# Two heads at once in a feature attention: maxima's rows handed over ahead of the query stores, and each query part stored once instead of once per use

## The chip, the cores and the metric

The kernel runs on one core of a Trainium2 chip. The metric is the device time of one execution in microseconds. A measured time is the median of several executions; one more execution was recorded by the hardware profiler, and every row shown below is from that one.

## The reference, cut to what matters

The program is a two-layer decoder block on x of 32 x 64 x 256 (2048 rows of 256, 16 tiles of 128 rows). It is six sublayers in a row: differential attention, feature attention, a selected low-rank feed-forward, a state-space layer, grouped attention and a mixture of experts. The change touches the second, and the end of the first, which prepares its first tiles. The second computes attention between features: the 64 rows of a sample are split into 8 heads of 8 rows, and each head has a 256 x 256 table of scores.

```python
def _L0_xattn_ref(q, k, v, W):           # q = layernorm(x), k = v = ctx, each (32, 64, 256)
    qh = q.reshape(B, H, D, Tq)          # H = 8 heads of D = 8 rows
    kh = k.reshape(B, H, D, Tk)
    vh = v.reshape(B, H, D, Tk)
    a = jnp.einsum('bhdq,bhdk->bhqk', qh, kh) * SCALE
    p = jax.nn.softmax(a, axis=-1)
    y = jnp.einsum('bhqk,bhdk->bhdq', p, vh).reshape(B, C, T)
    return jax.nn.selu(jnp.einsum('oc,bct->bot', W, y))
x = x + _L0_xattn_ref(layernorm(x), ctx, ctx, W)
```

A tile of 128 rows is two samples (b = 0, 1), so 16 heads, each with 256 x 256 scores.

## The kernel before, in words

**Scores from bf16 parts.** Queries and keys are float32, and the scores are made from three bf16 parts of each (high, middle, low). A product keeps six terms: the pairs of parts (0,0), (1,0), (2,0), (0,1), (1,1), (0,2) of query and key. The contraction of one head is then 6 terms x 8 rows = 48 rows. So the query stack has the parts in the order 0, 1, 2, 0, 1, 0 (`Q_TERMS`), the key stack in the order 0, 0, 0, 1, 1, 2 (`K_TERMS`). The stacks lie in SBUF with 48 rows of one head at partitions 0 to 47 and 48 rows of another at partitions 64 to 111 (two lanes), so that two heads are on the array at once. To bring the 8 rows of a head together from a tile's 128 partitions, each part goes through DRAM: `store` (line 176) writes a part to `q_parts` or `k_parts`, once for each of the six terms, and `load` (line 180) reads all 48 rows back, one DMA for each lane.

**Maxima.** The softmax needs each row's maximum ahead of the exponential. Head by head, TensorE first makes the scores with the queries on the output's partitions (`largest`, line 951), VectorE reduces them (`maximum`, line 783, two PSUM banks in turn), and GpSimd splits the 16 negated maxima of half a tile into three bf16 parts (`split_max`, lines 916 to 922). TensorE turns them into rows (`turn_max`, line 983), ScalarE copies these to SBUF (`max_to_rows`, line 832), and SyncE moves them by two DMAs into three more rows under the query stack (`max_to_stack`, line 747). There they meet three rows of ones in the key stack, so that the second product (`score`, line 956, 51 rows, keys on the partitions) has the maximum taken off, and ScalarE takes its exponential (line 838).

**The turn.** Each engine runs its own instruction list with semaphores between them, through `pipeline` (line 715): turns t = -1 to 16, of which -1 to 4 and 13 to 16 are unrolled and 5 to 12 lie in a loop. In turn t the engines work on several tiles:
- tile t + 3: x is normalised (VectorE line 113), split (GpSimd lines 905 to 911) and stored by SyncE (`store`, turns 1 to 12);
- tile t + 2: SyncE loads key and query stacks (`load`, turns 2 to 13);
- tile t + 1: `largest` and `maximum` for its 16 heads;
- tile t: `score`, exponentials, and the product with the values (`mix`, line 968);
- tile t - 1: output product (line 1036), SELU (ScalarE lines 861, 862, 872, then GpSimd lines 934 to 940, which end with x), and row statistics for the next sublayer (VectorE line 818, which waits for that x).

The 16 heads of a turn are eight groups, heads(0,0) to heads(0,3) and heads(1,0) to heads(1,3), with a `largest` and a `score` interleaved. All else of TensorE stands between two groups, in an order written by hand, and the lists of ScalarE and SyncE follow the same pattern. Two halves of maxima pass in each turn: `turn_max(t, 1)`, whose rows heads(1,0) of the same turn waits for, and `turn_max(t + 1, 0)`, whose rows heads(0,0) of the next turn waits for.

SyncE issues all DMAs in order. Before the change its turn is: load the context; wait for the maxima's rows of (t, 1) and issue their two DMAs; two key loads; wait until the tile's stores have landed; two query loads; six query stores; wait for the rows of (t + 1, 0) and issue their two DMAs.

## Time and profile before

| | us |
|---|---|
| median of 3 runs | 1390.13 |
| lowest, highest of them | 1388.1, 1390.63 |
| the profiled execution's own time | 1384.98 |
| its span (first to last instruction) | 1383.2 |
| feature attention in it, first matmul of line 951 to last of line 1036 | 252.0 to 500 |
| its mean granted TensorE clock | 0.962 of 2.4 GHz |

The profile names instructions by line and engine: PE is TensorE, PEld its weight loads, DVE VectorE, ACT ScalarE, POOL GpSimd, SP and SPq SyncE. "idle before <-releaser" is the time in which the engine waited ahead of the instruction, and what ended the wait.

### The profile page before, as it was taken

The numbers are of one execution on the slowest core, as the hardware profiler recorded it, in microseconds if no ns is written. First come the engines' busy times: TensorE is split into PE (matmuls) and PEld (weight loads), VectorE is DVE, ScalarE is ACT, GpSimd is POOL, SyncE is SP. The second block draws the span as 40 slices with busy tenths as digits, with TensorE's granted clock in tenths as the row PEclk, the third lists the DMA queues.
The fourth block names the chain that finished last, engine by engine and source line by source line (L and its number), as shares of the span: only waits on it lengthen the run. The fifth ranks groups of instructions, "written<-read, shape, count | busy, mean of one in ns | idle before, by whom it ended". The sixth has DMA issues, their size and how long they took to land. (4 is left out here: it accounts for less than half of the span.)

```text
span 1383.2 us, 27648 instructions
## 1 busy us (share of the span) xinstructions
PE 1231.3 (89%) x9980; PEld 970.1 (70%) x9996; DVE 987.4 (71%) x1869; ACT 705.4 (51%) x1457; POOL 455.3 (33%) x537
## 2 busy tenths in 40 slices
PE   4999998788888867889779999999997799999998
PEld 3776766233333335779657878787877799999998
DVE  4799987687777838788567777777866648655555
ACT  1555665287767854500156665656564364333332
POOL 1333543154444323457553424242322111112210
PEclk9999999699999989999899999999999899999999
DMA  5111025024333221000210000000000300000001
GB/s 177 32 26 35 24 69 134 23 61 106 87 82 84 53 65 45 1 0 0 90 56 4 4 7 4 8 4 8 4 5 0 93 24 25 24 24 24 2 1 62
DMA packets 64927, 54.52 MB, mean 39 GB/s; under 512 B 9192, under 2 KB 56904, under 8 KB 64456
## 3 DMA queue, kind: packets, MB, share of 16 engines
q1 hardware_dynamic: 64846, 53.42, 14.0%
q8 instruction: 53, 0.87, 0.3%
q14 instruction: 28, 0.23, 0.1%
HBM read 38.32 MB, written 14.68 MB: 38 GB/s over the span
## 5 line engine op out<-in xcount | busy, mean ns | idle before, releaser
L783 DVE TENSOR_REDUCE fa_neg_max<-psum 128x2 f32<-128x512 f32 x256 | 162.9, 686 | 38.9 <-PE psum L951 37.8
L838 ACT ACTIVATE fa_probs<-psum 128x1024 f32<-128x1024 f32 x128 | 130.9, 1024 | 45.2 <-PE psum L956 44.7
L1803 PE MATMUL psum<-mo_xT_high,mo_w_high 128*128 128x256 f32 x512 | 145.6, 284 | 2.4 <-DVE mo_xT_low L2631 2.2
L1803 PE MATMUL psum<-mo_xT_low,mo_w_high 128*128 128x256 f32 x512 | 145.2, 284 | 0.0
L1803 PE MATMUL psum<-mo_xT_high,mo_w_low 128*128 128x256 f32 x512 | 144.6, 282 | 0.0
L2463 ACT ACTIVATE mo_silu<-psum 128x256 f32<-128x256 f32 x128 | 49.0, 384 | 155.0 <-PE psum L1803 155.0
L2597 DVE TENSOR_TENSOR mo_mid<-mo_silu,psum 128x256 f32<-128x256 f32 x128 | 53.7, 420 | 92.8 <-ACT mo_silu L2463 92.7
L951 PE MATMUL psum<-stacks_k_stack,stacks_q_stack 48*128 48x256 bf16 x512 | 92.0, 290 | 29.1 <-DMA stacks_q_stack<-fa_max_rows 15.1
L1803 PEld LDWEIGHTS psum<-mo_xT_high,mo_w_high 128*128 128x128 f32 x512 | 97.4, 190 | 3.0 <-DVE mo_xT_low L2631 2.6
L1939 POOL TENSOR_TENSOR ga_probs<-ga_probs,ga_top 128x1024 f32<-128x1024 f32 x16 | 30.5, 1906 | 206.0 <-DVE ga_top L2093 206.0
L1803 PEld LDWEIGHTS psum<-mo_xT_low,mo_w_high 128*128 128x128 f32 x512 | 97.5, 190 | 0.0
L1803 PEld LDWEIGHTS psum<-mo_xT_high,mo_w_low 128*128 128x128 f32 x512 | 97.4, 190 | 0.0
L951 PEld LDWEIGHTS psum<-stacks_k_stack,stacks_q_stack 48*128 48x128 bf16 x512 | 32.7, 97 | 87.5 <-DVE fa_neg_max L783 42.3
L2404 POOL TENSOR_TENSOR mo_w_low<-mo_raw,mo_w_high 128x512 fp32r<-128x512 f32 x21 | 27.5, 1311 | 188.1 <-ACT mo_w_high L2438 188.1
L956 PE MATMUL psum<-stacks_q_stack,stacks_k_stack 51*128 51x256 bf16 x512 | 85.5, 283 | 0.3 <-DMA stacks_q_stack<-fa_max_rows 0.2
L1928 POOL TENSOR_TENSOR ga_q_scaled<-ga_q,ga_q_inv 128x1024 f32<-128x1024 f32 x32 | 70.1, 2190 | 38.2 <-ACT ga_q_inv L1970 38.2
L968 PE MATMUL psum<-fa_probs,fa_values 128*32 128x256 f32 x1024 | 71.8, 400 | 0.7 <-ACT fa_probs L838 0.6
L1963 ACT ACTIVATE ga_q_scaled<-ga_q 128x512 f32<-128x512 f32 x64 | 40.4, 632 | 62.6 <-DVE ga_q L2066 62.6
L1803 PE MATMUL psum<-mo_w_high,mo_mid_high 128*128 128x256 f32 x256 | 72.3, 282 | 0.0
L1803 PE MATMUL psum<-mo_w_low,mo_mid_high 128*128 128x256 f32 x256 | 71.9, 281 | 0.0
L1803 PE MATMUL psum<-mo_w_high,mo_mid_low 128*128 128x256 f32 x256 | 71.7, 280 | 0.0
L2262 PE MATMUL psum<-ga_w_o_high,ga_mixedT_high 128*128 128x256 f32 x256 | 63.2, 288 | 4.4 <-DVE ga_mixedT_low L2085 4.3
(419 smaller groups left out, 3584.2 us busy)
## 6 DMA issues: line engine op xcount, KB each, us to landing
k_parts<-da_k_parts SPq DMA_DIRECT2D x96, 64.0 KB, 2.0
q_parts<-stacks_parts SPq DMA_DIRECT2D x96, 64.0 KB, 2.0
stacks_q_stack<-q_parts SPq DMA_DIRECT2D x32, 192.0 KB, 4.1
stacks_k_stack<-k_parts SPq DMA_DIRECT2D x32, 192.0 KB, 3.4
x<-in_x SPq DMA_DIRECT2D x4, 512.0 KB, 5.5
da_context<-in_ctx SPq DMA_DIRECT2D x4, 512.0 KB, 7.9
fa_context<-in_ctx SPq DMA_DIRECT2D x16, 128.0 KB, 2.1
staged<-in_ga_w_q SPq DMA_DIRECT2D x1, 2048.0 KB, 10.1
```

The source lines that it names most:

```text
L783: nc.vector.tensor_reduce(neg_max[:, b, :, head_at(h)], ps[:, h % 2, :].rearrange("p (q k) -> p q k", q=2), AX.X, ALU.max, negate=True).th ...
L838: nc.scalar.activation(probs[:, g].rearrange("p h k q -> p h (k q)"), ps[:, 2 + 2 * (g % 2):4 + 2 * (g % 2), :], ACT.Exp).then_inc(exp_don ...
L951: return nc.tensor.matmul(ps[:, h % 2, q * E:(q + 1) * E], q_stack[lane, slot, b, h // LANES, q * P:(q + 1) * P], k_stack[lane, slot, b, h ...
L956: return nc.tensor.matmul(ps[:, 2 + h % 4, k * E:(k + 1) * E], k_stack[lane, slot, b, h // LANES, k * P:(k + 1) * P], q_stack[lane, slot, ...
L968: done = nc.tensor.matmul(ps[32 * c:32 * c + 32, 6, half * E:(half + 1) * E], values[:, slot, k, 8 * b + head_at(h), :], probs[:, h // 2, ...
L1803: done = nc.tensor.matmul(out, lhsT[i], rhs[j], start=start and k == 0, stop=stop and k == 2)
L1928: nc.gpsimd.tensor_tensor(q_scaled[:, columns].rearrange("p (h d) -> p h d", d=G_HD), q[:, columns].rearrange("p (h d) -> p h d", d=G_HD), ...
L1939: nc.gpsimd.tensor_tensor(probs[:], probs[:], top[:, :, None].to_broadcast([P, G_HEADS, SEQ]), ALU.subtract).then_inc(shifted, 1)
L1963: nc.scalar.activation(q_scaled[:, g * G_CHUNK:(g + 1) * G_CHUNK], q[:, g * G_CHUNK:(g + 1) * G_CHUNK], ACT.Square).then_inc(squares_ready, 1)
L2262: nc.tensor.matmul(ps[:, 6, 0:E], mixedT_high[:, h], weight[:, h], start=(h == 0 and weight is w_o_high), stop=False)
L2463: nc.scalar.activation(silu[:, j % 4], ps[:, j % 4, 0:2 * P], ACT.Silu).then_inc(silu_ready, 1)
L2597: nc.vector.tensor_tensor(mid[:, j % 4], silu[:, j % 4], ps[:, j % 4, 2 * P:4 * P], ALU.mult).then_inc(mid_ready, 1)
```

## The change

Two things are done at once.

**Order.** On SyncE the two DMAs of the maxima's rows of (t + 1, 0) are issued ahead of the query stores, not behind them. On TensorE `turn_max` goes one place forward in both halves: for (t, 1) ahead of heads(0,1) where it stood behind heads(0,1) and `turn_mixed`, and for (t + 1, 0) ahead of `turn_mixed(t, 0)`, not behind it. On ScalarE `max_to_rows(t, 1)` goes ahead of the second exponential of the turn, and `max_to_rows(t + 1, 0)` ahead of SELU's exponential (line 872).

**Stores and loads.** Each of the three query parts is stored once, so three stores for a tile and not six. The 48 rows of a lane are then read by three DMAs: rows of parts 0, 1, 2 (24 rows), of parts 0, 1 (16 rows), of part 0 (8 rows). That is six query loads for a tile and not two. The bytes loaded are the same, the bytes stored are half. Keys are as before. The first four tiles, prepared in the sublayer before, go the same way.

```diff
--- before.py
+++ after.py
@@ -147,8 +147,8 @@
 C_HEADS, C_HD = 8, 8
 HALF_HEADS = C_HEADS // 2
 PARTS = 3
-Q_TERMS, K_TERMS = (0, 1, 2, 0, 1, 0), (0, 0, 0, 1, 1, 2)
-TERMS = len(Q_TERMS)
+K_TERMS = (0, 0, 0, 1, 1, 2)
+TERMS = len(K_TERMS)
 MAX_ROW = TERMS * C_HD
 STACK_ROWS = MAX_ROW + PARTS
 LANES, LANE = 2, 64
@@ -183,7 +183,13 @@
             sp.dma_start(stack[LANE * lane:LANE * lane + MAX_ROW, slot].rearrange("p b h f -> p b (h f)"), of[:, :, lane]).then_inc(done, 16)
 
     def load_q(self, sp, tile, slot, done):
-        self.load(sp, "q_parts", self.q_stack, tile, slot, done)
+        of = self.dram["q_parts"][:, bass.ts(tile, 2 * C_HEADS), :].rearrange("p (b l h) f -> p b l (h f)", b=2, l=LANES)
+        for lane in range(LANES):
+            first = LANE * lane
+            for a in range(PARTS):
+                count = (PARTS - a) * C_HD
+                sp.dma_start(self.q_stack[first:first + count, slot].rearrange("p b h f -> p b (h f)"), of[0:count, :, lane]).then_inc(done, 16)
+                first += count
 
     def load_k(self, sp, tile, slot, done):
         self.load(sp, "k_parts", self.k_stack, tile, slot, done)
@@ -304,17 +310,17 @@
                 store_keys(n)
             for n in range(RING):
                 sp.wait_ge(q_split, n + 1)
-                for term, a in enumerate(Q_TERMS):
-                    stacks.store(sp, "q_parts", n, term, stacks.parts[:, n, a]).then_inc(q_stored, 16)
+                for a in range(PARTS):
+                    stacks.store(sp, "q_parts", n, a, stacks.parts[:, n, a]).then_inc(q_stored, 16)
             sp.wait_ge(k_stored, 16 * TERMS * STORED)
             for n in range(RING):
-                sp.wait_ge(q_stored, 16 * TERMS * RING)
+                sp.wait_ge(q_stored, 16 * PARTS * RING)
                 stacks.load_q(sp, n, n, stacked)
                 stacks.load_k(sp, n, n, stacked)
             for n in range(STORED, TILES):
                 store_keys(n)
             sp.wait_ge(context_loaded, 16 * TILES // RING)
-            sp.wait_ge(stacked, 16 * 2 * LANES * RING)
+            sp.wait_ge(stacked, 16 * (LANES + LANES * PARTS) * RING)
             sp.wait_ge(k_stored, 16 * TERMS * TILES)
             sp.wait_ge(ones_loaded, 16 * LANES)
             sp.wait_ge(loaded, LOADS)
@@ -708,7 +714,7 @@
         mixed_turned, mixed_c_ready, projected, channels_read = (sem(n) for n in ("mixed_turned", "mixed_c_ready", "projected", "channels_read"))
         exp_below_ready, selu_parts, selu_ready, negative_ready, selu_sum, x_ready, stats_done = (
             sem(n) for n in ("exp_below_ready", "selu_parts", "selu_ready", "negative_ready", "selu_sum", "x_ready", "stats_done"))
-        LOADS, STORES = 2 * LANES * 16, TERMS * 16
+        LOADS, STORES = (LANES + LANES * PARTS) * 16, PARTS * 16
 
         block = scope.enter_context(nc.Block())
 
@@ -755,8 +761,8 @@
 
             def store(t, slot):
                 sp.wait_ge(split_done, t + 1)
-                for term, a in enumerate(Q_TERMS):
-                    stacks.store(sp, "q_parts", t + 3, term, parts[:, slot, a]).then_inc(stored[slot], 16)
+                for a in range(PARTS):
+                    stacks.store(sp, "q_parts", t + 3, a, parts[:, slot, a]).then_inc(stored[slot], 16)
 
             def turn(t, ring, rounds, valid):
                 if valid(t + 3):
@@ -767,10 +773,10 @@
                     max_to_stack(t, ring(0), 1)
                 if valid(t + 2) and started(t, 2):
                     load(t, ring(2), rounds(2))
+                if valid(t + 1):
+                    max_to_stack(t + 1, ring(1), 0)
                 if valid(t + 3) and started(t, 1):
                     store(t, ring(3))
-                if valid(t + 1):
-                    max_to_stack(t + 1, ring(1), 0)
 
             pipeline(sp, turn)
 
@@ -847,9 +853,8 @@
                 if valid(t - 1):
                     take_mixed(t - 1, 1)
                 if valid(t):
+                    max_to_rows(t, 1)
                     exponentials(t, 0, 1)
-                if valid(t):
-                    max_to_rows(t, 1)
                     exponentials(t, 0, 2)
                 if valid(t - 1):
                     act.wait_ge(mixed_turned, t)
@@ -865,13 +870,13 @@
                     take_mixed(t, 0)
                 if valid(t):
                     exponentials(t, 1, 1)
+                if valid(t + 1):
+                    max_to_rows(t + 1, 0)
                 if valid(t - 1):
                     act.wait_ge(selu_parts, t)
                     if started(t, 2):
                         act.wait_ge(selu_ready, t - 1)
                     nc.scalar.activation(exp_below[:], below[:], ACT.Exp, scale=-1.0).then_inc(exp_below_ready, 1)
-                if valid(t + 1):
-                    max_to_rows(t + 1, 0)
                 if valid(t):
                     exponentials(t, 1, 2)
                 if valid(t + 1):
@@ -1012,12 +1017,12 @@
                 heads(0, 0)
                 if valid(t - 1):
                     mix(t - 1, ring(-1), 1, 1)
+                if valid(t):
+                    pe.wait_ge(values_ready, t + 1)
+                    turn_max(t, 1)
                 heads(0, 1)
                 if valid(t - 1):
                     turn_mixed(t - 1, 1)
-                if valid(t):
-                    pe.wait_ge(values_ready, t + 1)
-                    turn_max(t, 1)
                 heads(0, 2)
                 if valid(t - 1):
                     if valid(t):
@@ -1038,8 +1043,6 @@
                 if valid(t):
                     mix(t, ring(0), 0, 1)
                 heads(1, 1)
-                if valid(t):
-                    turn_mixed(t, 0)
                 if valid(t + 1):
                     if isinstance(t, int) and t == -1:
                         pe.wait_ge(loaded, 32)
@@ -1048,6 +1051,8 @@
                     elif valid(t):
                         pe.wait_ge(max_rows_ready, 2 * t + 2)
                     turn_max(t + 1, 0)
+                if valid(t):
+                    turn_mixed(t, 0)
                 heads(1, 2)
                 if valid(t + 1):
                     pe.wait_ge(context_ready[ring(1)], 16 * rounds(1) + 16)
@@ -2763,8 +2768,8 @@
 
 def decoder(nc, dram):
     with ExitStack() as ctx:
-        for name in ("q_parts", "k_parts"):
-            dram[name] = nc.dram_tensor(name, (TERMS * C_HD, BATCH * C_HEADS, E), BF16, kind="Internal").ap()
+        for name, count in (("q_parts", PARTS), ("k_parts", TERMS)):
+            dram[name] = nc.dram_tensor(name, (count * C_HD, BATCH * C_HEADS, E), BF16, kind="Internal").ap()
         core = Core(nc, ctx, dram)
         with ExitStack() as scope:
             stacks = FeatureStacks(core, scope)
```

## Rows read from the trace of the kernel before

**Rows 1.** The page's costliest groups: what, xcount | busy us, mean ns | idle before, releaser
```profile
L783 DVE TENSOR_REDUCE fa_neg_max<-psum 128x2 f32<-128x512 f32 x256 | 162.9, 686 | 38.9 <-PE psum L951 37.8
```

**Rows 2.** Waits, 262 to 482 us: us in total, times, longest us
```profile
PE psum L951 <- DMA stacks_q_stack<-fa_max_rows: 15.1, 12, 2.2
...
DVE row_stats L818 <- POOL x L940: 7.5, 13, 0.7
```

**Rows 3.** Timeline of TensorE, line 1036 of seven turns: start us, us, what
```profile
284.92 0.70 PE L1036 MATMUL psum<-fa_mixed_c,fa_w_out 128*128 128x256 f32 x2
...
326.86 0.70 PE L1036 MATMUL psum<-fa_mixed_c,fa_w_out 128*128 128x256 f32 x2
...
341.35 0.70 PE L1036 MATMUL psum<-fa_mixed_c,fa_w_out 128*128 128x256 f32 x2
...
358.93 0.70 PE L1036 MATMUL psum<-fa_mixed_c,fa_w_out 128*128 128x256 f32 x2
...
448.75 0.70 PE L1036 MATMUL psum<-fa_mixed_c,fa_w_out 128*128 128x256 f32 x2
...
463.67 0.70 PE L1036 MATMUL psum<-fa_mixed_c,fa_w_out 128*128 128x256 f32 x2
...
477.35 0.70 PE L1036 MATMUL psum<-fa_mixed_c,fa_w_out 128*128 128x256 f32 x2
```

**Rows 4.** Timelines of ScalarE, SyncE and TensorE where turn 6 begins late
```profile
345.44 0.35 ACT L832 CAST fa_max_rows<-psum 24x256 bf16<-24x256 f32 x1
...
342.88 4.70 SPq L178 DMA_DIRECT2D q_parts<-stacks_parts  x6
347.71 1.58 SPq L747 DMA_DIRECT2D stacks_q_stack<-fa_max_rows  x2
...
347.30 1.07 PE L968 MATMUL psum<-fa_probs,fa_values 128*32 128x256 f32 x16
350.59 0.28 PE L951 MATMUL psum<-stacks_k_stack,stacks_q_stack 48*128 48x256 bf16 x1 [2.22 <-DMA stacks_q_stack<-fa_max_rows]
```

**Rows 5.** Windows: us, busy us (x) of PE, PEld, DVE, ACT, POOL, clock, DMA, GB/s
```profile
352.00:356.00 4.00, 4.00 (x28) 1.99 (x24) 2.96 (x7) 2.65 (x5) 0.67 (x1) 0.50 0.02 4
```

**Rows 6.** Windows, the same columns, while a tile's loads run
```profile
374.00:375.00 1.00, 1.00 (x20) 0.37 (x12) 0.97 (x2) 1.00 (x3) 0.00 (x0) 1.00 1.01 223
```

**Rows 7.** Timelines of five engines where turn 7 begins with little wait
```profile
362.71 0.41 ACT L872 ACTIVATE fa_exp_below<-fa_below 128x256 f32<-128x256 f32 x1
363.02 0.35 ACT L832 CAST fa_max_rows<-psum 24x256 bf16<-24x256 f32 x1
...
376.41 0.41 ACT L872 ACTIVATE fa_exp_below<-fa_below 128x256 f32<-128x256 f32 x1
...
367.08 0.22 POOL L922 TENSOR_TENSOR fa_max_parts<-fa_max_rest,fa_max_parts 128x16 bf16<-128x16 f32 x1
...
366.40 0.43 DVE L818 BATCH_NORM_STATS2 row_stats<-x  x1 [0.65 <-POOL x L940]
366.74 0.40 DVE L113 TENSOR_SCALAR fa_rows<-x,fa_mean,fa_rstd 128x256 f32 x1
367.07 2.47 DVE L783 TENSOR_REDUCE fa_neg_max<-psum 128x2 f32<-128x512 f32 x4
...
366.26 0.28 PE L951 MATMUL psum<-stacks_k_stack,stacks_q_stack 48*128 48x256 bf16 x1 [0.30 <-DMA stacks_q_stack<-fa_max_rows]
...
367.81 0.28 PE L951 MATMUL psum<-stacks_k_stack,stacks_q_stack 48*128 48x256 bf16 x1
...
363.39 1.58 SPq L747 DMA_DIRECT2D stacks_q_stack<-fa_max_rows  x2
```

**Rows 8.** SyncE's issues of the query loads: ns min/median/max; then landing of line 183
```profile
L183 SPq DMA_DIRECT2D stacks_q_stack<-q_parts x32: 316/379/587, 208.0 to 464.6; - x32
...
DMA to landing us min/median/max: 2.8/3.9/8.9
```

**Rows 9.** The same for the query stores of line 178
```profile
L178 SPq DMA_DIRECT2D q_parts<-stacks_parts x96: 546/598/1347, 191.2 to 453.6; - x96
```

## The prediction

> **What bounds the kernel now.** I read the waits of the feature attention first. Most of them are engines with room waiting for the two that share the work, VectorE (16 maxima a turn at 0.69 us [rows 1]) and TensorE. One stands out: TensorE waited 15.1 us in 12 turns for the DMAs of the maxima's rows, and nothing fills it [rows 2]. Then I took the length of a turn from one instruction that comes once in each, line 1036 [rows 3]. From turn 4 (326.86) to turn 12 (448.75) eight turns took 121.89 us, 15.24 each; turn 13 took 14.92 and turn 14, with no query store ahead of it, 13.68. Turns 2 to 4 are hardly over that: (326.86 - 284.92) / 3 = 13.98.
>
> A stalled turn shows why [rows 4]. The rows' copy to SBUF ends at 345.79, but SyncE is in six query stores from 342.88 to 347.58, issues the two DMAs at 347.71 to 349.29, and TensorE starts the next turn 1.30 us behind that, at 350.59. Its own work had ended at 348.37. So stores that nobody waits for soon stand ahead of rows that TensorE waits for now. This stall of 2.22 us cost more than itself: the granted clock was 0.50 in 352 to 356 [rows 5], which is the lower of the two levels, 1.2 GHz, and turn 6 came to 358.93 - 341.35 = 17.58 us [rows 3].
>
> Turn 7 is what a turn looks like without the stall [rows 7]. I measure from E, the start of SELU's exponential, line 872. E = 362.71; the next is at 376.41, a turn of 13.70. TensorE waited 0.30 us for the rows here, and it wasn't what counted: VectorE waited 0.65 us for x of GpSimd's SELU (statistics at E + 3.69), normalised, and began the maxima at M = 367.07 = E + 4.36. All four ran back to back, so TensorE was ahead of it. From M to the next E are 9.34 us. The floor of a turn is thus 4.36 + 9.34, and its first half is a chain ScalarE line 872, GpSimd, VectorE.
>
> **The change, step by step.**
>
> *Rows ahead of the stores.* On ScalarE the copy of (t + 1, 0) goes ahead of line 872, so it takes the latter's place at E and is done at E + 0.34 (line 872 starts 0.31 behind the copy's place, and the copy is as long [rows 7]). `turn_max` is one place forward on TensorE, so the copy finds its input there. SyncE issues E + 0.36 to E + 1.94 (1.58 [rows 7]), and 1.29 later (363.39 + 1.58 to 366.26 [rows 7]) TensorE may begin: E + 3.23. Its own work ends at 348.37, with E = 345.44 - 0.31 = 345.13, so E + 3.24 [rows 4]. The stall goes to nothing.
>
> *What is late next.* Line 872 moves back by a copy, 0.31. Everything behind it in the chain follows: x, statistics, normalisation, maxima at M = E + 4.67. TensorE needs M only 0.4 after its start, E + 3.65, so this chain and not the rows sets the turn. Its price is the whole 0.31 a turn; below it could only be nothing, if VectorE's wait for x ended by something else, and the 0.65 us wait ahead of line 818 [rows 7], 7.5 us in 13 turns [rows 2], says that it doesn't. I take 0.31.
>
> *`turn_max(t, 1)` ahead of heads(0,1).* It now waits for GpSimd's last of four splits. That ends at 367.30 = E + 4.59 [rows 7], with the shift E + 4.90. TensorE gets there after heads(0,0) and a `mix`, 367.81 - 366.26 = 1.55 us after its start, E + 4.79 to 4.95. Two small matmuls later it is about E + 5.2. Heads(0,1) needs VectorE's first maximum anyway, which was 367.81 - 367.07 = 0.74 after M, now E + 5.41. So it costs nothing, with 0.2 us to spare; without that cover it costs what it is late by. What it saves, later between groups, VectorE's pace hides. The same holds for `turn_max(t + 1, 0)` ahead of `turn_mixed`, 0.2 us of delay to a division that comes behind four maxima. In turn 0 there is no `mix` to cover GpSimd's splits: below 0.5 us, once.
>
> *Three stores for six.* SyncE's 4.70 us become about 2.35, E + 2.0 to E + 4.4, behind the rows. They have to have landed by the query loads of the next turn, which stand behind the rows of (t, 1) and two key loads, about E + 8.5. Even with the loads' 3.9 us [rows 8] they have by E + 8.3: hidden. Behind SyncE's waits stand the context load (four tiles' ring, turns of slack) and the loads.
>
> *Six loads for two.* The trace has no query load of 24, 16 or 8 rows. Issue: below, the shortest of 48 rows, 0.32 each; above, a store's median 0.60 [rows 9] and once its slowest turn, 4.70 / 6 = 0.78 [rows 4]. I take the like row, 0.38 [rows 8], with register work 0.45: 2.7 us, E + 8.5 to E + 11.2. At 0.78 it ends at E + 13.2, still ahead of the next rows at 14.01 + 0.36. Landing: median 3.9, up to 8.9 [rows 8]. TensorE needs the stack at 14.01 + 3.23 = E + 17.24, so with 3.9 there are 2.1 us in hand. The engines are full while a tile's loads run (DMA share 1.01 [rows 6]), but this load is spread more thinly in time and no stores follow. I take nothing.
>
> The Trainium skill ("DMA: Bandwidth & Descriptors", Why a DMA increments its semaphore by 16 and not by 1) says that a DMA is split over the largest number of engines up to 16 that divides both sides' outermost sizes. By that, 48 rows go over 16 engines, but 24, 16 and 8 over 12, 16 and 8, and the busiest carry 2 + 1 + 1 = 4 rows where they carried 3; an estimate from it is a query load a third longer, 5.2 for 3.9 us, inside the same 2.1 us of slack. No row here shows engine by engine which one is true.
>
> *The sublayer before.* Four tiles: 12 stores less at 0.60 and 16 loads more at about 0.42, 7.2 against 6.7 us of SyncE. Key stores still follow to its end. Nothing.
>
> **The sum,** on the profiled execution (1384.98, its span 1383.2):
> - turns 5 to 12: 121.89 becomes 8 x (4.67 + 9.34) = 112.1: -9.8, in which the halved clock goes too, as it followed the stall
> - turn 13: 14.92 becomes about 13.7, as turn 14: -1.2
> - turns 2 to 4, with 13.98 already at the new length of 14.0: 0; turn 0: +0.2
>
> Together -10.8, so 1374.2 there. The median of the runs shown is 5.15 above that execution, with nothing to say where, and I carry the difference over: 1390.13 - 10.8 = 1379.3.
>
> **Rivals.**
>
> *Floor not raised.* If line 872's shift is hidden, a turn is 13.70 and the eight give 121.89 - 109.6 = 12.3, turn 13 its 1.2: 1376.6. For it: the profile infers what ended a wait, and 0.65 us of one could be something else's. Against: the chain's times fit it in both halves.
>
> *The stack comes late (slower).* The six small query loads land later than two large ones, and TensorE meets `stacked` at heads(0,0) in place of the rows. It decides from a landing of 6.0 us behind the last issue (E + 17.24), and lengthens the turn from 7.0 on, as M leaves TensorE 1.0 more. At the 8.9 that some landed in [rows 8] a turn is 14.01 + 1.9 = 15.9: over eight turns 127.3, which is +5.4, turns 2 to 4 and 13 add four times 1.9 less 1.2, so +11.8 in all: 1402. For it: full DMA engines, three times the issues. Against: half the store traffic, and the median. The rule on the number of engines above speaks for it, and gives it part of its chance.
>
> *The gain is eaten at `turn_max(t, 1)`.* TensorE waits there in order, now 0.2 us from GpSimd's end. Each turn that GpSimd, or SyncE behind a wait, is late by L beyond that costs L - 0.2; with L = 1.1 (its four splits once over, as when VectorE's last maximum were late) 0.9 x 12 is 10.8 and the change gives nothing: 1390. For it: GpSimd's four splits come right behind SELU. Against: this delay starts from the same chain that holds VectorE back.
>
> *The stall is not the order's.* If the rows' two DMAs were slow themselves, or the lower clock came without the stall, the reorder would give half: 1385. Against it: 1.3 us from issue to start both in the stalled turn and in the other [rows 4, 7].
>
> **How the numbers follow.** Forecast 0.58, floor not raised 0.14, half the gain 0.11, eaten 0.09, stack late 0.08. The predicted time is 1379.3; its own range is 1376 to 1383 (0.31 missed either way on eleven turns is 3.4). The wider range takes in the floor not raised below and the half gain above, and 2 us on either side for the difference of 5.15 that I carried over, which moves by as much between the runs shown: 1373 to 1388, with eaten and stack late outside. A measurement of this kernel can tell 0.2%, 2.8 us, from no change. Faster 0.83 (the first three), same 0.09, slower 0.08.
>
> **What would show it.** The wait of line 951 for the rows' DMAs goes from 15.1 us to under 3. Turns 5 to 12 are 14.0 us by line 1036, not 15.24, and the clock is full from 280 to 490. VectorE's wait for x (7.5 us) grows to about 11. SyncE issues the rows within 0.1 us of their copy, stores in 2.4 us and query loads in 2.7. It is wrong if a wait on the query loads stands at the turn's start, if TensorE waits at line 983, or if turns are 13.7.

## The result, and the profile after

| | us |
|---|---|
| before, median of 4 runs | 1390.38 (1388.1 to 1390.65) |
| changed, median of 4 runs | 1376.76 (1374.82 to 1378.37) |
| ratio, 95% interval | 0.9905, 0.9885 to 0.9925 |
| changed, profiled execution: time, span | 1378.37, 1376.6 |

The kernel became 1% faster: -13.6 us between the medians, where -10.8 had been forecast. The time, 1376.76 for a forecast of 1379.3, is inside the likeliest case's own range. (Of the runs in the experiments below, two with a far lower clock, 1986 us at 0.555 and 1442 us at 0.828, are left out of medians and ratios.) The profiled executions differ by only 1378.37 - 1384.98 = -6.6; the last part of this section shows where the other 4.3 us of the stage's gain went.

First the waits of feature attention (us in total, times, longest), from 262 to 482 us.

```profile
DVE row_stats L824 <- POOL x L945: 11.6, 14, 0.9
PEld psum L988 <- POOL fa_max_parts L927: 4.7, 8, 0.6
...
PE psum L988 <- POOL fa_max_parts L927: 1.1, 3, 0.7
PE psum L956 <- DMA stacks_q_stack<-fa_max_rows: 0.9, 2, 0.5
PEld psum L961 <- DMA stacks_q_stack<-fa_max_rows: 0.4, 1, 0.4
```

Line 956 is `largest`, which was line 951. Its 15.1 us of waiting for the maxima's rows [rows 2] are 0.9 now, with 0.4 at the score product beside it. VectorE's wait for x has grown from 7.5 to 11.6 us, and a new wait for the split maxima stands at `turn_max` (line 988). Now the turns, by the output product (line 1041), at places that answer to those of [rows 3].

```profile
326.94 0.70 PE L1041 MATMUL psum<-fa_mixed_c,fa_w_out 128*128 128x256 f32 x2
...
438.87 0.70 PE L1041 MATMUL psum<-fa_mixed_c,fa_w_out 128*128 128x256 f32 x2
...
452.62 0.70 PE L1041 MATMUL psum<-fa_mixed_c,fa_w_out 128*128 128x256 f32 x2
...
466.32 0.70 PE L1041 MATMUL psum<-fa_mixed_c,fa_w_out 128*128 128x256 f32 x2
```

| turns | before | after | forecast |
|---|---|---|---|
| 2 to 4, each | 13.98 | 13.80 | 13.98 |
| 5 to 12, together | 121.89 | 438.87 - 326.94 = 111.93 | 112.1 |
| 13 | 14.92 | 13.75 | 13.7 |
| 14 | 13.68 | 13.70 (466.32 - 452.62) | 13.7 |

(A turn is named as in [rows 3]: 326.94 stands for 326.86 there, and 13.75 and 13.70 are the last two distances.) The eight turns that were 13.69 to 17.58 long are now 13.82 to 13.97, but for one of 14.41.

The turn that answers to [rows 7], one on from that of [rows 4], on four engines (start us, us, what [idle before <-releaser]).

```profile
358.51 0.35 ACT L838 CAST fa_max_rows<-psum 24x256 bf16<-24x256 f32 x1
358.76 0.41 ACT L879 ACTIVATE fa_exp_below<-fa_below 128x256 f32<-128x256 f32 x1
...
372.46 0.35 ACT L838 CAST fa_max_rows<-psum 24x256 bf16<-24x256 f32 x1
...
358.88 1.48 SPq L753 DMA_DIRECT2D stacks_q_stack<-fa_max_rows  x2
360.56 2.65 SPq L178 DMA_DIRECT2D q_parts<-stacks_parts  x3
...
364.23 1.59 SPq L753 DMA_DIRECT2D stacks_q_stack<-fa_max_rows  x2
366.02 0.86 SPq L183 DMA_DIRECT2D stacks_k_stack<-k_parts  x2
366.98 2.32 SPq L191 DMA_DIRECT2D stacks_q_stack<-q_parts  x6
...
362.46 0.43 DVE L824 BATCH_NORM_STATS2 row_stats<-x  x1 [0.91 <-POOL x L945]
362.81 0.41 DVE L113 TENSOR_SCALAR fa_rows<-x,fa_mean,fa_rstd 128x256 f32 x1
363.13 2.47 DVE L789 TENSOR_REDUCE fa_neg_max<-psum 128x2 f32<-128x512 f32 x4
...
361.69 0.28 PE L956 MATMUL psum<-stacks_k_stack,stacks_q_stack 48*128 48x256 bf16 x1
...
363.42 0.28 PE L988 MATMUL psum<-fa_ident_bf,fa_max_parts 128*24 128x128 bf16 x2
363.87 0.28 PE L956 MATMUL psum<-stacks_k_stack,stacks_q_stack 48*128 48x256 bf16 x1 [0.17 <-DVE fa_neg_max L789]
```

The copy of the maxima's rows takes the place of SELU's exponential (E = 358.51) and SyncE issues their DMAs 0.02 us behind its end. TensorE begins the turn at E + 3.18 and waits for nothing. What is late is VectorE, 0.91 us for x. The maxima begin at E + 4.62, and 9.33 later comes the next copy: a turn of 13.95. The clock says the same (busy us of PE, PEld, DVE, ACT, POOL, granted clock, DMA share, GB/s):

```profile
330.00:380.00 50.00, 44.46 (x522) 19.33 (x522) 41.88 (x83) 39.64 (x61) 27.49 (x60) 1.00 0.30 77
380.00:430.00 50.00, 44.06 (x515) 19.29 (x514) 40.83 (x79) 39.85 (x62) 23.23 (x54) 1.00 0.34 85
```

Before, the same two windows had 0.93 and 0.97, with stretches at 0.50 [rows 5]; after, all of 280 to 480 is at 1.00.

**The sublayers behind.** They hold the same instructions in both kernels. The DMA of `fs_w_in` starts the next sublayer, that of `mo_w_route` stands 580 us further on. Before:

```profile
L1215 SPq DMA_DIRECT2D fs_w_in<-in_ff_w_in x1: 415/415/415, 506.2 to 506.2; - x1
...
L2376 SPq DMA_DIRECT2D mo_w_route<-in_mo_w_route x1: 469/469/469, 1083.2 to 1083.2; - x1
```

After:

```profile
L1220 SPq DMA_DIRECT2D fs_w_in<-in_ff_w_in x1: 410/410/410, 495.3 to 495.3; - x1
...
L2381 SPq DMA_DIRECT2D mo_w_route<-in_mo_w_route x1: 469/469/469, 1076.5 to 1076.5; - x1
```

The stage ended 10.9 us sooner (506.2 to 495.3), and from there the way was 581.2 us and not 577.0. Of the twelve profiled executions of this study five took 877 to 879 us from `fs_w_in` to the end of the span, six 881 to 882.5 and one 886. Of these two, before had a granted clock of 0.87 in the first 100 us of that, after 0.84. But this clock doesn't sort the twelve: `x_later` had 0.86 there and took 882.4, `gap_six_stores` 0.84 and took 878.3. Timed runs of one kernel fall apart alike: the six of `order_only` below took 1372.7, 1373.8 and 1374.2 at a clock of 0.964 and 1378.5, 1378.6 and 1378.6 at 0.959. The 12 runs of before in the first group of experiments even lie from 1385.59 to 1398.68; whether that spread stands behind the stage too, or in it, isn't shown, as one of its executions alone was traced. So in the traces the way behind the stage carries 4 to 5 us that the change doesn't explain, and below the stage is compared first, by the eight turns 5 to 12.

### The profile page after: what moved, and what is told of

Read it like the earlier page. It is cut to its first block and busy times, and to the rows that moved or that the text cites. A ratio compares the mean times of both kernels' runs of the same rounds, so it can differ in the third digit from the quotient of the medians.

```text
span 1376.6 us, 27662 instructions
## 1 busy us (share of the span) xinstructions
PE 1236.7 (90%) x9996; PEld 972.7 (71%) x9996; DVE 984.4 (72%) x1869; ACT 703.9 (51%) x1457; POOL 455.2 (33%) x537
## 5 line engine op out<-in xcount | busy, mean ns | idle before, releaser
L956 PE MATMUL psum<-stacks_k_stack,stacks_q_stack 48*128 48x256 bf16 x512 | 95.4, 287 | 22.3 <-DVE fa_neg_max L789 15.5
L961 PE MATMUL psum<-stacks_q_stack,stacks_k_stack 51*128 51x256 bf16 x512 | 89.3, 279 | 0.0
```

Of the source, the lines that this page charges most:

```text
L956: return nc.tensor.matmul(ps[:, h % 2, q * E:(q + 1) * E], q_stack[lane, slot, b, h // LANES, q * P:(q + 1) * P], k_stack[lane, slot, b, h ...
L961: return nc.tensor.matmul(ps[:, 2 + h % 4, k * E:(k + 1) * E], k_stack[lane, slot, b, h // LANES, k * P:(k + 1) * P], q_stack[lane, slot, ...
```

## The experiments

Medians and ratios (95% interval) are against the kernel before in runs on the same chip, 11 or 12 runs of it in each of the three groups (1389.24, 1389.33 and 1391.29).

| kernel | median | ratio | turns 5 to 12 |
|---|---|---|---|
| before | 1389.24 | 1 | 121.89 |
| the change (second measurement) | 1376.99 | 0.9899 (0.9864 to 0.9933) | 111.98 |
| `order_only` | 1376.38 | 0.9900 (0.9870 to 0.9931) | 111.92 |
| `parts_only` | 1380.68 | 0.9935 (0.9910 to 0.9960) | 116.25 |
| `selu_first` | 1374.98 | 0.9901 (0.9873 to 0.9929) | 109.98 |
| `syncE_only` | 1370.85 | 0.9873 (0.9842 to 0.9904) | 110.00 |
| `x_later` | 1407.65 | 1.0131 (1.0087 to 1.0176) | 132.82 |
| `stats_in_gap` | 1367.97 | 0.9844 (0.9807 to 0.9881) | 107.06 |
| `stats_in_gap_syncE_only` | 1371.00 | 0.9867 (0.9829 to 0.9904) | 108.64 |
| `gap_turn_max_behind` | 1370.07 | 0.9845 (0.9812 to 0.9878) | 106.32 |
| `gap_six_stores` | 1371.31 | 0.9865 (0.9833 to 0.9898) | 109.68 |

**order_only: the new order with the old stores and loads.** The kernel before with the order of all three engines as in the change, with six stores and two loads. Its TensorE and ScalarE parts, in short (SyncE's stands under `syncE_only`):

```diff
+                    turn_max(t, 1)
                 heads(0, 1)
...
-                    turn_max(t, 1)
...
+                if valid(t + 1):
+                    max_to_rows(t + 1, 0)
                 if valid(t - 1):
                     act.wait_ge(selu_parts, t)
```

> The order of the change alone: rows ahead of the stores on SyncE, turn_max and the copies one place forward; six stores and two query loads a tile as before. My theory: what limited a turn was a ring through SyncE in which TensorE's start waited for stores, so the order alone takes it away, and the turn is set by SELU's exponential, GpSimd and VectorE at 4.67 + 9.34 = 14.0 us, as in the changed kernel; the six stores (4.7 us) end at about E + 6.6 and delay the rows of (t, 1) by 1.2 us, which heads(1,0), 2 us later, doesn't see. Turns 5 to 12: 112 us, against 121.9 before. Total about 11 below the kernel before, ratio 0.990 to 0.993. Rival, the traffic: halving the stores is what pays; then turns stay near 15 us and the ratio is above 0.998.

Measured: 1376.38, and 111.92 for the eight turns, as the whole change to 0.01 us. SyncE, where the stores now stand behind the rows:

```profile
358.92 1.48 SPq L747 DMA_DIRECT2D stacks_q_stack<-fa_max_rows  x2
360.60 4.65 SPq L178 DMA_DIRECT2D q_parts<-stacks_parts  x6
...
366.02 1.60 SPq L747 DMA_DIRECT2D stacks_q_stack<-fa_max_rows  x2
```

Six stores take 2.0 us more than three, and the rows of (t, 1) start 1.8 us later than in the changed kernel (366.02 for 364.23), but nobody waits for them yet. The order alone, all five moves of it, makes the gain; which of the moves does is asked below, on the changed kernel.

**parts_only: the new stores and loads with the old order.** The changed kernel with the five moves undone, so this is what is left of the change:

```diff
-                for term, a in enumerate(Q_TERMS):
+                for a in range(PARTS):
...
+            for a in range(PARTS):
+                count = (PARTS - a) * C_HD
```

> Three stores and six query loads a tile, but the order of before on all engines. My theory: the ring through SyncE stays closed and only gets shorter. From the kernel before, ring of one turn: 3.6 us from TensorE's start to the copy of (t, 1), 1.5 rows, 0.3 and 0.9 key loads, 0.2 and 1.1 query loads, 0.3 and 4.7 stores, 0.1 and 1.6 rows, 1.3 landing: 15.6. With six loads 2.3 to 2.9 and three stores 2.2 it is 14.3 to 14.9. Turns 5 to 12: about 115 (114 to 119), TensorE still waits for the rows' DMAs, about 0.5 us a turn. Ratio 0.993 to 0.996. Rival, the traffic: as fast as the changed kernel, 0.990. Rival, the loads come late: slower than before.

Measured: 116.25, the ratio 0.9935. Three stores are enough to shorten the line ahead of the rows, but not to take it away: the wait for the rows is still 9.6 us in 12 turns. The longest, 2.46 us, comes in the turn where SyncE was slow with the six loads; the seven others of turns 5 to 12 are 0.32 to 1.06. The timelines of SyncE, then TensorE:

```profile
338.36 3.34 SPq L191 DMA_DIRECT2D stacks_q_stack<-q_parts  x6
341.98 2.19 SPq L178 DMA_DIRECT2D q_parts<-stacks_parts  x3
344.30 1.59 SPq L753 DMA_DIRECT2D stacks_q_stack<-fa_max_rows  x2
...
347.19 0.39 PE L957 MATMUL psum<-stacks_k_stack,stacks_q_stack 48*128 48x256 bf16 x1 [2.46 <-DMA stacks_q_stack<-fa_max_rows]
```

And the window right behind, with the columns of the windows above:

```profile
348.00:352.00 4.00, 4.00 (x32) 1.75 (x28) 2.41 (x4) 2.47 (x3) 0.99 (x2) 0.50 0.02 4
```

The rows' DMAs end on SyncE at 345.89, and TensorE starts 1.30 us later, as in [rows 4]. The clock is at 0.50 here, TensorE busy all 4.00 us, and that turn is 17.97 us long; the seven others are 13.68 to 14.43. Loads and stores share one queue with the rows, so here the six loads' issue is what the rows wait for as much as the stores.

**selu_first: SELU's exponential back ahead of the copy.**

```diff
-                if valid(t + 1):
-                    max_to_rows(t + 1, 0)
                 if valid(t - 1):
                     act.wait_ge(selu_parts, t)
...
                     nc.scalar.activation(exp_below[:], below[:], ACT.Exp, scale=-1.0).then_inc(exp_below_ready, 1)
+                if valid(t + 1):
+                    max_to_rows(t + 1, 0)
```

> The changed kernel, but on ScalarE SELU's exponential stands ahead of the copy of (t + 1, 0), as in the kernel before. My theory: the chain exponential, GpSimd, VectorE gets back its 0.31 us, so the maxima begin at E + 4.36; the rows allow TensorE to start at E + 3.54, still ahead. turn_max(t, 1) stands ahead of heads(0,1), which then begins at E + 5.3 where VectorE wants it at E + 5.1, so 0.1 to 0.2 may be lost. A turn 13.7 to 13.85, turns 5 to 12 110 to 111 us (changed kernel 111.9), 1 to 3 us below the changed kernel, ratio to before about 0.988. Rival, the rows set the turn: 0.31 us later a turn, 14.25 and more.

Measured: 109.98 for the eight turns, 13.67 to 13.72 each but for turn 9, which took 14.15. ScalarE and VectorE of one turn:

```profile
369.11 0.41 ACT L877 ACTIVATE fa_exp_below<-fa_below 128x256 f32<-128x256 f32 x1
369.42 0.34 ACT L838 CAST fa_max_rows<-psum 24x256 bf16<-24x256 f32 x1
...
372.81 0.43 DVE L824 BATCH_NORM_STATS2 row_stats<-x  x1 [0.66 <-POOL x L945]
373.15 0.40 DVE L113 TENSOR_SCALAR fa_rows<-x,fa_mean,fa_rstd 128x256 f32 x1
373.47 2.48 DVE L789 TENSOR_REDUCE fa_neg_max<-psum 128x2 f32<-128x512 f32 x4
```

The maxima begin at 373.47 = E + 4.36 again, as in [rows 7], and VectorE's wait is back to 0.66. (111.93 - 109.98) / 8 = 0.24 us a turn: that is the price of the copy ahead of the exponential, and nothing on the other side pays for it. In the whole time it doesn't show, since the intervals are 0.3% wide to each side.

**syncE_only: one of the moves alone.** The changed kernel, three stores and six loads included, with TensorE's and ScalarE's order as before. Of the order this is what is left of the change:

```diff
                     load(t, ring(2), rounds(2))
+                if valid(t + 1):
+                    max_to_stack(t + 1, ring(1), 0)
                 if valid(t + 3) and started(t, 1):
                     store(t, ring(3))
-                if valid(t + 1):
-                    max_to_stack(t + 1, ring(1), 0)
```

> The changed kernel with only SyncE's order new; TensorE and ScalarE in the order of before (turn_max behind heads(0,1) and behind turn_mixed, the copies behind the exponentials). My theory: as SELU's exponential first, and without turn_max in front of heads(0,1): a turn is 4.36 + 9.34 = 13.70, turns 5 to 12 109.6 us, 3 to 4 us below the changed kernel, ratio to before 0.987. The change's moves on TensorE and ScalarE are then a loss. Rival, the moves on TensorE and ScalarE bring the rows early enough: without them TensorE waits for the rows and turns are above 14.0.

Measured: 110.00, as in `selu_first`, and 1370.85, the lowest of its group. `parts_only` (116.25) is this kernel without the swap on SyncE, so the swap is worth 6.25 us beside three stores. The moves of `turn_max` and of the copy of (t, 1) add nothing to it, and that of the copy of (t + 1, 0) costs 0.24 a turn. The swap alone beside six stores was not run, so that it makes up the gain of `order_only` by itself is likely but not shown.

**changed_again: the changed kernel beside the versions below.** No edit; it is the yardstick of the second group.

> The changed kernel itself once more, to stand beside the others on the same chip. Turns 5 to 12 take 111.9 us as before; ratio 0.990.

Measured: 1376.99 and 111.98, as in the first measurement (1376.76, 111.93), so in the changed kernel the eight turns repeat to 0.05 us where the medians repeat to 0.2. Of the kernel before there is one trace.

**x_later: the chain lengthened on GpSimd.** In the changed kernel GpSimd's `split_max(t + 1, 1)` goes ahead of the add into x, so that `turn_max` may start sooner and x comes later. It asks which of the two ends of GpSimd's list is the one that counts.

```diff
+                if valid(t + 1):
+                    split_max(t + 1, 1)
                 if valid(t - 1):
                     pool.wait_ge(selu_sum, t)
                     nc.gpsimd.tensor_tensor(core.x[:, t - 1, :], core.x[:, t - 1, :], selu[:], ALU.add).then_inc(x_ready, 1)
-                if valid(t + 1):
-                    split_max(t + 1, 1)
```

> The changed kernel, but GpSimd's split of the maxima (t + 1, 1) stands ahead of the addition into x, not behind it. A dose for the chain to VectorE: the split can't begin before the last maximum, E + 3.1, and takes 1.2 us, so x is ready 1.2 to 1.3 us later. My theory (VectorE's wait for x sets the turn): a turn 13.95 + 1.2 = 15.2, turns 5 to 12 121 to 122 us, ratio to before about 1.0. Rival (the chain has slack, the turn is set by TensorE): the x wait grows but turns stay at 14.

Measured: 132.82, ratio 1.0131. VectorE of one turn, then windows of two others:

```profile
356.71 0.43 DVE L824 BATCH_NORM_STATS2 row_stats<-x  x1 [2.08 <-POOL x L948]
...
406.00:411.00 5.00, 5.00 (x39) 1.91 (x38) 3.75 (x8) 3.33 (x4) 2.07 (x5) 0.53 0.69 158
...
423.00:428.00 5.00, 5.00 (x42) 2.21 (x38) 4.06 (x8) 3.33 (x4) 1.76 (x5) 0.53 0.61 157
```

The direction was right, the size was not. Turns 3, 4 and 8, at the full clock, are 14.9 to 15.1 (expected 15.2), 1.0 to 1.2 over the changed kernel's; the other seven of turns 5 to 12 are 15.5 to 17.5, with the clock at its lower level for a part of each, which none of the theories had in it. VectorE now waits 24.3 us for x, and TensorE behind VectorE's first maximum up to 2.1 us a turn. A later x makes the turn longer by about as much, so the chain through x is the one that sets the turn.

**stats_in_gap: the chain taken out.** VectorE takes the statistics of one tile earlier and the normalisation from the start of its turn to the middle, where it waits for TensorE anyway. GpSimd splits maxima first:

```diff
                 for b in range(2):
                     for g in range(4):
+                        if b == 1 and g == 0 and valid(t - 2):
+                            dve.wait_ge(x_ready, t - 1)
+                            nc.vector.bn_stats(core.row_stats[:, t - 2, :], core.x[:, t - 2, :]).then_inc(stats_done, 1)
+                        if b == 1 and g == 0 and valid(t + 3) and started(t, 1):
+                            dve.wait_ge(split_done, t)
+                            ln.normalise(rows[:], t + 3).then_inc(rows_ready, 1)
...
-                if valid(t - 1):
-                    dve.wait_ge(x_ready, t)
-                    nc.vector.bn_stats(core.row_stats[:, t - 1, :], core.x[:, t - 1, :]).then_inc(stats_done, 1)
...
             def turn(t, ring, rounds, valid):
-                if valid(t + 3) and started(t, 1):
-                    split(t + 3, ring(3), rounds(3))
...
                 if valid(t + 1):
                     split_max(t + 1, 0)
+                if valid(t + 3) and started(t, 1):
+                    split(t + 3, ring(3), rounds(3))
```

`split_max(t + 1, 1)` stands ahead of the add into x, and ScalarE waits for the last tile's SELU before it writes `above` again.

> The changed kernel with the chain cut: VectorE does the statistics (a tile later) and the normalisation ahead of the ninth maximum of a turn, where it waits 1.19 us for TensorE anyway, GpSimd splits the maxima ahead of the query split and of the addition into x. My theory: nothing of SELU is in the turn any more; TensorE starts at E + 3.23 and VectorE 0.42 behind it, so a turn is 3.65 + 9.34 = 13.0 us, turns 5 to 12 104 us, about 8 us less than the changed kernel, ratio to before 0.982 to 0.985. Rival, TensorE or ScalarE is the bound at about 13.7: no gain over the kernel with SELU's exponential first.

Measured: 107.06, every turn 13.38 long; 1367.97. VectorE across one turn:

```profile
357.73 1.29 DVE L789 TENSOR_REDUCE fa_neg_max<-psum 128x2 f32<-128x512 f32 x2 [0.56 <-PE psum L961]
359.37 1.29 DVE L789 TENSOR_REDUCE fa_neg_max<-psum 128x2 f32<-128x512 f32 x2 [0.35 <-PE psum L961]
...
363.50 0.42 DVE L812 BATCH_NORM_STATS2 row_stats<-x  x1
363.84 0.40 DVE L113 TENSOR_SCALAR fa_rows<-x,fa_mean,fa_rstd 128x256 f32 x1
364.78 1.29 DVE L789 TENSOR_REDUCE fa_neg_max<-psum 128x2 f32<-128x512 f32 x2 [0.55 <-PE psum L961]
```

The statistics wait for nobody, and all of VectorE's waits are for TensorE. The maxima begin at 357.73, 3.60 us behind the copy (354.13), where 3.65 was expected. But from there to the next copy it is 9.78, not 9.34: a new wait of 0.35 stands ahead of the third maximum, where heads(0,1) comes behind `turn_max(t, 1)`. So the forecast of 13.0 was 0.4 short. Against the change, measured beside it, the eight turns are 111.98 - 107.06 = 4.9 us shorter.

**stats_in_gap_syncE_only: the same on `syncE_only`.** The edits of `stats_in_gap`, and on ScalarE and TensorE the old order:

```diff
-                if valid(t + 1):
-                    max_to_rows(t + 1, 0)
                 if valid(t - 1):
                     act.wait_ge(selu_parts, t)
...
+                if valid(t + 1):
+                    max_to_rows(t + 1, 0)
```

> The same cut of the chain on the kernel in which only SyncE's order is new. The copy of (t + 1, 0) is then behind SELU's exponential, so TensorE starts at E + 3.54 and VectorE at E + 3.96. My theory: here the moves on ScalarE and TensorE count, which cost 0.3 us a turn while the chain set it: a turn is 13.3, turns 5 to 12 106.4 us, 2.4 us more than with the order of the changed kernel. Rival, the copy's place never counts: both equal.

Measured: 108.64, turns of 13.57 to 13.60 (13.3 expected). With the chain through x gone, the moves on TensorE and ScalarE together are worth (108.64 - 107.06) / 8 = 0.20 us a turn, where with the chain the same moves cost (111.93 - 110.00) / 8 = 0.24.

**gap_turn_max_behind: the first half's move undone.** In `stats_in_gap`, `turn_max(t, 1)` and its copy go back behind heads(0,1) and the second exponential.

```diff
-                if valid(t):
-                    pe.wait_ge(values_ready, t + 1)
-                    turn_max(t, 1)
                 heads(0, 1)
                 if valid(t - 1):
                     turn_mixed(t - 1, 1)
+                if valid(t):
+                    pe.wait_ge(values_ready, t + 1)
+                    turn_max(t, 1)
```

> The kernel with statistics in the gap, and turn_max(t, 1) and its copy moved back behind heads(0,1) and the second exponential, as in the kernel before; turn_max(t + 1, 0) and its copy stay forward. With the chain cut, VectorE waited 0.35 us for heads(0,1) because turn_max and a mix stood in front of it. My theory: turn_max ahead of heads(0,1) costs its 0.21 us once TensorE sets this place, so a turn is 13.2 (13.38 before), turns 5 to 12 105.4 us, 2 us less. Rival, the rows of (t, 1) then reach heads(1,0) late, as on SyncE they stand behind stores and the context load: 13.4 and more.

Measured: 106.32, 13.29 a turn, 0.09 less than `stats_in_gap` and 0.09 more than expected. So of the two halves only (t + 1, 0) gains by its move, (108.64 - 106.32) / 8 = 0.29 us a turn. The ratio, 0.9845, is that of `stats_in_gap` to a ten-thousandth: the two are the fastest versions, and which is the better the whole times don't say.

**gap_six_stores: does the second part of the change matter now?** `stats_in_gap` with six stores and two loads.

```diff
-                for a in range(PARTS):
-                    stacks.store(sp, "q_parts", t + 3, a, parts[:, slot, a]).then_inc(stored[slot], 16)
+                for term, a in enumerate(Q_TERMS):
+                    stacks.store(sp, "q_parts", t + 3, term, parts[:, slot, a]).then_inc(stored[slot], 16)
```

> The kernel with statistics in the gap, but with six stores and two query loads a tile. In the changed kernel the stores' number didn't count, as they delay only the rows of (t, 1), with 0.9 us in hand. Here the turn is shorter: stores end at E + 6.7, context load 7.1, rows issued 8.7, landed 10.0, and heads(1,0) wants them at E + 9.6 (3.65 + 9.78 - 3.8). My theory: about 0.4 us of waiting a turn for the rows at heads(1,0), a turn 13.7 to 13.9, turns 5 to 12 109.6 to 111, 3 to 4 us more in all; halving the stores pays only once the order has made SyncE the next bound. Rival, no difference here either: 13.38.

Measured: 109.68. Five turns are 13.38 as with three stores, three are 14.0, 14.5 and 14.3. One of these, SyncE and TensorE:

```profile
355.29 1.48 SPq L747 DMA_DIRECT2D stacks_q_stack<-fa_max_rows  x2
356.97 5.50 SPq L178 DMA_DIRECT2D q_parts<-stacks_parts  x6
...
363.23 1.60 SPq L747 DMA_DIRECT2D stacks_q_stack<-fa_max_rows  x2
...
366.24 0.28 PE L955 MATMUL psum<-stacks_k_stack,stacks_q_stack 48*128 48x256 bf16 x1 [1.02 <-DMA stacks_q_stack<-fa_max_rows]
```

The stores, 5.50 us here and not 4.65, push the rows of (t, 1) to 364.83, and heads(1,0) waits 1.02 us. The expected total was met, but the way to it wasn't: it is not a little in each turn, it is some turns whose stores issue slowly. The three turns with a wait for the rows (0.55, 1.02 and 0.82 us) had stores of 4.96, 5.50 and 4.79 us; stores of 4.34 to 4.38 us (at 371.44, 399.13, 412.49 and 425.88) had none behind them. In this version three stores are worth 2.6 us, in the changed kernel nothing.

## Why the prediction was right

**Rows ahead of the stores (stall to nothing): right.** TensorE was forecast to be able to begin at E + 3.23, and began at E + 3.18 with no wait. The rows' wait went from 15.1 to 1.3 us and the lower clock went with it, in `order_only` with six stores as well. The swap on SyncE is the move that does it beside three stores (`parts_only` against `syncE_only`). The rival that the stall is not the order's falls with it. The eight turns of before were 11.55 us of waiting for the rows, 3.4 us of the lower clock (worked out in the last section), and 13.36 each for the rest; now they are 13.99, and this 0.63 a turn is what the next limit took back.

**Line 872 moves back (0.31 a turn): right in kind, 0.06 too much.** I took the whole distance from [rows 7], where the copy starts 0.31 behind the exponential; in the new order the exponential starts 0.25 behind the copy (358.51, 358.76), since what follows an exponential starts 0.31 behind it and what follows a copy 0.25. The maxima came at E + 4.62, not 4.67. `selu_first` gave back 0.24 a turn, so this price was real, and "floor not raised", with its 13.70 a turn, is refuted for the changed kernel: VectorE's wait for x is what sets it.

**`turn_max` at nothing: right, with the margin forecast.** The last split ended at 363.36 (E + 4.85; forecast 4.90), the small matmuls began at 363.42, and heads(0,1) behind them still waited 0.17 us for VectorE, where 0.2 had been given. So TensorE does wait at line 988, 4.7 us of its weight loads in 8 turns and 1.1 of its matmuls in 3, and I had written that a wait there would make the forecast wrong. That sign was too strict: a wait with a later one behind it costs nothing. "Eaten at `turn_max(t, 1)`" therefore happened in its place but not in its size. Once it was in the open: turn 0 waited 0.66 us there, forecast below 0.5.

**Stores and loads: right that they gain nothing and cost nothing.** In the loop three stores took 2.15 to 2.65 us (2.35 forecast), six loads mostly 2.32 (2.7 forecast): a load of 24, 16 or 8 rows has a median issue of 0.32 us where 0.38 had been taken, and with its register work 2.32 / 6 = 0.39 for 0.45. Not every turn was so: the first two of the loop took 3.5 us for the six, turn 8 2.87 and turn 13 3.30. No wait for the stack stands at a turn's start, so "the stack comes late", and with it the longer load by the number of engines, did not decide anything here; its landing was not measured by itself.

**The sum: right in the stage (-10.9 for -10.8), in part because errors cancel.** Turns 5 to 12 -9.96 for -9.8: the 0.06 a turn would be -0.5, and turn 9 gave back 0.4. That turn, the first of the second pass through the loop, is that much longer with either order, by a pause of VectorE that ends for no reason the profile has:

```profile
391.16 0.41 DVE L113 TENSOR_SCALAR fa_rows<-x,fa_mean,fa_rstd 128x256 f32 x1 [0.38 <-issue]
```

Where the normalisation is off the chain (`stats_in_gap`) no turn is longer. Turn 13 -1.17 for -1.2. Turns 2 to 4 -0.5 for 0: their 13.98 hid short waits in them, and I had read it as the new floor because it was near. Against that, the product of turn 1 came 0.62 later (285.54 for 284.92), where 0.2 had been given to turn 0. The profiled execution as a whole missed its 1374.2 by 4.2, all of it behind the stage; that is the 581.2 against 577.0 shown above.

**The offset carried over (5.15 us): not explained, and of no help here.** The measured median is 2.6 below 1379.3, and 2.6 above the 1374.2 that would stand without the offset. The profiled execution of before took the shorter way through the later sublayers and its four runs are 3 to 6 us above it, as if they took the longer; the changed kernel's profiled run took the longer one and lies at the top of its runs. The median's -13.6 is thus -11 that is shown by traces, and some 3 within what the later sublayers and the intervals leave open (0.2% either way); that 1376.76 fell into a range of 1376 to 1383 owes something to luck. What puts a run on the one or the other way stays open. So does whether the other runs of before, up to 14 us longer than the traced one, had more of the stall and the lower clock in the stage itself.

**What was not seen.** The change holds a loss beside its gain. All three engines were moved for one stall that, beside three stores, one swap on SyncE takes away, and the copy on ScalarE costs 8 x 0.24 = 2 us of the 12 that were to be had. That could be read in [rows 7] (0.31 given, no row that gives it back), and the forecast has it as a term, but not as an edit to leave out.

## What to carry to other kernels

In an in-order queue that issues DMAs, put what an engine waits for now ahead of what is needed a turn later: beside three stores that swap took 6.3 us from eight turns. Halving the stores (with six loads for two) took 5.6 in the old order, nothing in the new and 2.6 once the turn had become shorter. An instruction that is moved forward pushes its neighbour back: look whether the neighbour's chain is the one that sets the turn, as the same moves cost 0.24 us a turn with it and brought 0.20 without it. Compare the stage and not the program where the rest of the program moves by more than the edit.

## What the runs showed of the hardware

In the kernel before, a turn that waits over 1 us for the rows, at the full clock, is its wait and 13.36 us, to 0.01:

| turn of before | 5 | 6 | 7 | 8 | 9 | 10 | 11 | 12 |
|---|---|---|---|---|---|---|---|---|
| length | 14.49 | 17.58 | 13.69 | 14.92 | 16.85 | 14.95 | 14.73 | 14.68 |
| wait for the rows | 1.13 | 2.22 | 0.30 | 1.56 | 2.08 | 1.58 | 1.37 | 1.31 |
| the rest | 13.36 | 15.36 | 13.39 | 13.36 | 14.77 | 13.37 | 13.36 | 13.37 |

The two that stand out are those in which the granted clock fell to 0.50 ([rows 5] for turn 6; 397.00 to 399.00 in turn 9), and what the lower clock costs on top of the wait is 15.36 - 13.36 = 2.0 and 14.77 - 13.36 = 1.4 us. In `parts_only` the seven turns at the full clock give 13.36 or 13.37 as well, and the one with the wait of 2.46 us has 17.97 - 2.46 - 13.36 = 2.1 on top. In the kernel before it fell at the waits of 2.08 and 2.22 us, not at those of 1.13 to 1.58. But the length of one wait doesn't tell: in `x_later` the clock fell behind one of 1.56 and stayed full behind one of 1.64. The row of turn 9 in the kernel before, then two rows and windows of `x_later`, with the columns of the windows above:

```profile
396.65 0.39 PE L951 MATMUL psum<-stacks_k_stack,stacks_q_stack 48*128 48x256 bf16 x1 [2.08 <-DMA stacks_q_stack<-fa_max_rows]
...
340.81 0.28 PE L957 MATMUL psum<-stacks_k_stack,stacks_q_stack 48*128 48x256 bf16 x1 [1.56 <-DVE fa_neg_max L789]
342.00:346.00 4.00, 4.00 (x32) 1.90 (x34) 3.27 (x7) 2.62 (x4) 1.34 (x2) 0.50 0.56 152
...
358.11 0.28 PE L957 MATMUL psum<-stacks_k_stack,stacks_q_stack 48*128 48x256 bf16 x1 [1.64 <-DVE fa_neg_max L789]
359.00:363.00 4.00, 3.51 (x41) 1.58 (x39) 3.75 (x8) 3.26 (x4) 1.54 (x4) 1.00 0.67 166
```

The time of an issue on SyncE is not constant: in the changed kernel six query loads took 3.5 us in turns 5 and 6 and mostly 2.3 later, in `syncE_only` they took 2.4 in turn 5 already, and six stores took 4.34 to 5.50 us in the loop of `gap_six_stores`. The stall of 2.46 us in `parts_only` and the three in `gap_six_stores` all came behind such slow issues. Why they are slow isn't shown.
